# A four-layer graph network on one core: the masked minimum of a score tile taken in two halves of 512 columns

## What is computed

```python
# layer 0
h   = relu(fa[:, :, None, :] + fb[:, None, :, :])      # 1024 x 1024 pairs, 64 features
att = einsum('bijo,o->bij', h, W2)
att = softmax(att + where(adj > 0, 0.0, NEG_INF), axis=-1)
out = einsum('bij,bjc->bic', att, feat)
# layer 1: the same with leaky_relu(vu + iv), yita in the place of W2,
# and a small linear step behind it
```

## Time and profile before

| what | value |
|---|---|
| median of three runs | 5095.22 us |
| the profiled execution, its own time | 5096.0 us |
| its span in the trace | 5094.1 us |
| PE / DVE / ACT / POOL busy over the span | 4584.2 / 4798.2 / 4747.6 / 3856.7 us |
| TensorE's granted clock, mean | 0.983 of full |
| masked minima (L471) of tiles 0 to 127 start | 55.3 to 3460.2 us |

### The profile page before, as it was taken

The page is one execution under the profiler, slowest core; times in us unless marked ns, Lnnn a source line. Parts: engine busy times, 40 slices in busy tenths (PEclk is TensorE's granted clock), DMA queues, the critical chain, the costliest instruction groups (busy, mean ns, idle before and its releaser), DMA issues. The chain is left out here.

```text
span 5094.1 us, 118654 instructions
## 1 busy us (share of the span) xinstructions
PE 4584.2 (90%) x48920; PEld 1810.2 (36%) x48920; DVE 4798.2 (94%) x5489; ACT 4747.6 (93%) x5779; POOL 3856.7 (76%) x3611
## 2 busy tenths in 40 slices
PE   7888888888888999999999999998789999999998
PEld 2222222222222223232323323234445555555554
DVE  7999999999999999999999999996579999999998
ACT  7999999999999999999999999996779999999997
POOL 8999999999999999999999999993603223322333
PEclk9999999999999999999999999998879999999999
DMA  1000010000000000000000000003210111001100
GB/s 53 32 28 30 32 32 26 32 32 29 30 32 32 18 10 12 12 12 10 12 12 12 9 12 12 12 10 73 69 26 16 24 25 24 16 24 24 24 16 12
DMA packets 154140, 121.74 MB, mean 24 GB/s; under 512 B 118854, under 2 KB 120646, under 8 KB 153606
## 3 DMA queue, kind: packets, MB, share of 16 engines
q1 hardware_dynamic: 152902, 114.10, 8.0%
q10 hardware_dynamic: 704, 0.07, 0.0%
HBM read 86.87 MB, written 18.87 MB: 21 GB/s over the span
## 5 line engine op out<-in xcount | busy, mean ns | idle before, releaser
L200 POOL TENSOR_SCALAR a_hid_p<-a_BLOS,a_PHI,a_PLO 128x1024 f32<-128x1024 f32 x2720 | 3196.9, 1222 | 89.0 <-PE apsS L330 82.5
L459 DVE SCALAR_TENSOR_TENSOR a_hid_p<-apsB,a_THI,a_hid_p 128x1024 f32<-128x1024 f32 x2560 | 3074.7, 1273 | 16.5 <-POOL a_hid_p L200 14.6
L330 PE MATMUL apsS<-a_hid_p,a_sel_high 128*32 128x512 f32 x10880 | 2633.9, 597 | 169.9 <-ACT a_hid_a L367 96.9
L330 PE MATMUL apsS<-a_hid_a,a_sel_high 128*32 128x512 f32 x6144 | 1913.3, 597 | 47.1 <-ACT a_hid_a L367 24.9
L330 PE MATMUL apsS<-a_hid_a,a_sel_low 128*32 128x512 f32 x5504 | 1680.2, 597 | 109.1 <-ACT a_hid_a L367 61.7
L367 ACT ACTIVATE a_hid_a<-a_BHI,a_ALH 128x1024 f32<-128x1024 f32 x1536 | 1690.7, 1146 | 0.0
L367 ACT ACTIVATE a_hid_a<-a_BLO,a_ALH 128x1024 f32<-128x1024 f32 x1376 | 1534.6, 1146 | 0.0
L330 PEld LDWEIGHTS apsS<-a_hid_p,a_sel_high 128*32 128x32 f32 x10880 | 587.8, 109 | 938.5 <-issue 535.1
L761 PE MATMUL m3S<-xT,Q 64*128 64x512 f32 x2048 | 594.3, 655 | 28.1 <-ACT x_even L805 14.1
L330 PEld LDWEIGHTS apsS<-a_hid_a,a_sel_high 128*32 128x32 f32 x6144 | 419.7, 109 | 560.1 <-issue 303.7
L330 PEld LDWEIGHTS apsS<-a_hid_a,a_sel_low 128*32 128x32 f32 x5504 | 374.7, 109 | 647.9 <-issue 325.9
(11 more groups left out here) (187 smaller groups left out, 3870.7 us busy)
## 6 DMA issues: line engine op xcount, KB each, us to landing
a_adj_in<-adj SPq DMA_DIRECT2D x64, 512.0 KB, 3.7
mask_rows<-a_mask SPq DMA_DIRECT2D x64, 256.0 KB, 2.2
a_mask<-mask_rows SPq DMA_DIRECT2D x64, 256.0 KB, 2.7
maskb<-mask_rows SPq DMA_DIRECT2D x64, 256.0 KB, 3.0
mask<-mask_rows SPq DMA_DIRECT2D x64, 256.0 KB, 2.8
Xr<-x_odd SPq DMA_DIRECT2D x128, 64.0 KB, 2.1
out<-yn SPq DMA_DIRECT2D x64, 32.0 KB, 1.5
x_even<-x SPq DMA_DIRECT2D x1, 256.0 KB, 2.7
```

The lines of the kernel that those rows point to most:

```text
L200: gp.tensor_scalar(hid_p[:, at % RING_P, :], BLOS[:, g % 2, :], PHI[:, g % 2, m:m + 1], PLO[:, g % 2, m:m + 1], ALU.min, ALU.max).then_inc ...
L330: last = pe.matmul(psS[32 * q:32 * q + 32, h * HALF:(h + 1) * HALF], sel[:, 28 - 4 * p:60 - 4 * p], unit, start=s == 0 and layer == 0, sto ...
L459: dve.scalar_tensor_tensor(out=hid_p[:, at % RING_P, :], in0=psB[:, :], scalar=THI[:, g % 2, m:m + 1], in1=hid_p[:, at % RING_P, :], op0=A ...
```

## The change

`masked_min` becomes two operations of 512 columns. The first waits for a new semaphore `half_scored`, which the fourth matmul of the tile's last set raises, the second for `hid_used` as before. Each writes its row minimum to a column of its own (`half_lowest`), and a third VectorE operation, a 128x1 `tensor_tensor` with `min`, waits for both and writes `lowest(k)`; it raises `low_ready`, for which ScalarE's exponentials now wait. `min_ready` counts two for each tile. On TensorE, set 0 of the next tile and `key_term` wait for each half of the minimum in front of their own half. SyncE and GpSimd wait for the same event as before, by doubled counts.

```diff
@@ gpsimd / sync: the same event, counted twice
-                    gp.wait_ge(min_ready, k - 1)
+                    gp.wait_ge(min_ready, 2 * (k - 1))
@@ def key_term(k)
-                pe.wait_ge(min_ready, k)
                 for h, side in enumerate(halves):
+                    pe.wait_ge(min_ready, 2 * (k - 1) + h + 1)
@@ def hidden_set(k, s)
-                if s == 0 and k >= 1:
-                    pe.wait_ge(min_ready, k)
                 for h in range(n // HALF):
+                    if s == 0 and k >= 1:
+                        pe.wait_ge(min_ready, 2 * (k - 1) + h + 1)
                     for q, p, kind in units:
...
+                    if s == SETS - 1 and h == 0:
+                        last.then_inc(half_scored, 1)
                 last.then_inc(hid_used, 1)
@@ def exponentials(k)
-                act.wait_ge(min_ready, k + 1)
+                act.wait_ge(low_ready, k + 1)
@@ def masked_min(k)
-                dve.wait_ge(hid_used, (k + 1) * SETS)
+                dve.wait_ge(half_scored, k + 1)
...
-                dve.tensor_tensor_reduce(out=Z, in0=psS[:, :], in1=mask[:, k % 2, :], scale=1.0, scalar=-LOWEST,
-                                         op0=ALU.add, op1=ALU.min, accum_out=lowest(k)).then_inc(min_ready, 1)
+                for h in range(2):
+                    if h == 1:
+                        dve.wait_ge(hid_used, (k + 1) * SETS)
+                    dve.tensor_tensor_reduce(out=Z[:, columns(h)], in0=psS[:, columns(h)], in1=mask[:, k % 2, columns(h)],
+                                             scale=1.0, scalar=-LOWEST, op0=ALU.add, op1=ALU.min,
+                                             accum_out=half_lowest(k, h)).then_inc(min_ready, 1)
+                dve.wait_ge(min_ready, 2 * (k + 1))
+                dve.tensor_tensor(lowest(k), half_lowest(k, 0), half_lowest(k, 1), ALU.min).then_inc(low_ready, 1)
```

More of the change, by code:

```diff
@@ L63, in additive_layers @@
     lowest, halfc = lambda k: small[:, k % 2:k % 2 + 1], small[:, 8:9].to_broadcast([P, tiles])
+    half_lowest = lambda k, h: small[:, 2 + 2 * (k % 2) + h:3 + 2 * (k % 2) + h]
+    columns = lambda h: slice(h * HALF, h * HALF + HALF)
     per_tile = lambda ap: ap.rearrange("p (t c) -> p t c", c=C)
@@ L132, in additive_layers @@
         bounds_ready, keys_placed = sem("bounds_ready"), sem("keys_placed")
+        half_scored, low_ready = sem("half_scored"), sem("low_ready")
         turned, copied_low, copied_high = sem("turned"), sem("copied_low"), sem("copied_high")
@@ L153, in _ @@
                 else:
-                    sp.wait_ge(min_ready, k - 1)
+                    sp.wait_ge(min_ready, 2 * (k - 1))
                     sp.wait_ge(mask_stored[k % 2], 16 * (M // 2))
```

## The result

The changed kernel takes 5259.0 us (median of 4 runs, 5252.85 to 5259.97) where the kernel before takes 5093.16 (4 runs beside it): a ratio of 1.0316, 95% interval 1.0303 to 1.033. That is 166 us slower. The forecast was 5101, the range ended at 5119: the prediction is wrong, and not by a little.

The account below looks back on a forecast made before the run. The prediction took VectorE and ScalarE, in turns, as the bound: d of 0.25 us per minimum less waits given back, +4.3 us in layer 0 and +1.7 in layer 1, so 5095.2 + 6 = 5101 us; range 5088 to 5119.

Parts of the forecast that it names:

- What bounds the kernel: Layers 0 and 1: no engine alone; VectorE and ScalarE take turns in cycles of eight tiles, TensorE has slack.
- d: VectorE's added time per tile from minimum's start to next merged unit: +0.25 us, bounds +0.14 and +0.46.
- the early start: First half starts up to 0.86 us before `hid_used`; of a wait w the change takes back min(w, 0.61).
- TensorE's slack in layer 1: TensorE was said to have 19 to 26 us of slack in eight tiles of layers 0 and 1.
- The price of the halves, of the wait and of the 0.07 of the join: On VectorE: 0.61 first half, 0.69 to the second's end, 0.03 wait, 0.07 join; next merged unit at 1.40.
- Operations on one column take 0.14 and follow each other at 0.07: Price of the join on VectorE: from rows 10, next merged unit 0.07 us after the join's start.
- the upper bound of the join at 0.17: The join's share in the upper bound of d, 0.72 + 0.72 + 0.17 - 1.15 = +0.46 us.
- Rival B: VectorE's three pieces do not overlap, d = 0.46, costing places 3 to 7: +22 us, 5117; chance 0.25.
- Rival A: The join's wait on VectorE is free, d = 0.14: -3 us, 5092; chance 0.15.
- Rival C: All VectorE waits given back at the minimum are on the path: -19 us, 5076; chance 0.10.
- The signs I had named: Next merged unit at 1.40, minimum's idle under 30 us, ScalarE's exponential wait above 40, layer 0 cycle 216.0; other distance: wrong d.

Follow-up runs that it names:

- reduce_join: The changed kernel with the join as a tensor_reduce over one 128x2 SBUF input, not a tensor_tensor with two SBUF inputs: 5099.47 us, ratio to before 1.001.
- halves_late: reduce_join without the early start: both halves wait for `hid_used`, `half_scored` is gone; 5117.56 us, ratio 1.0051.
- chained: Two halves and no join: the second half waits for the first one's minimum and takes it as its initial value; 5105.81 us, ratio 1.0031.
- the pair of unused operations: The kernel before plus one unused 128x1 VectorE operation behind each minimum: two-input tensor_tensor 5228.34 us (1.026), tensor_reduce over two SBUF columns 5094.69 (1.0005).

## Why the prediction was wrong, point by point

**What bounds the kernel: right in the main.** VectorE and ScalarE take turns in cycles of eight tiles, and the early start does give back time on it. Three kernels that differ in d and in the early start came out near the sums built on this: reduce_join +6.1 us (forecast +6), halves_late +25 (20), chained +13.7 (12.4), the sums in brackets with the d of tile 29. The split by layer is less good. Layer 1 took +0.1, +11.4 and +4.0 us, where the sums say +1.7, +10 and +4.1; layer 0 took +6.6, +13.5 and +13.4, where they say +4.3, +10 and +8.3. In layer 0 something of 2 to 5 us is missing from the sum, so that +6.1 for a forecast of +6 is in part luck, and no run shows what. One reading of the rows was off: TensorE's slack in layer 1 is 214.60 - 196.63 = 18 us, not 19, on which nothing hangs.

**The price of the halves, of the wait and of the 0.07 of the join: right.** d of a join with one SBUF input is 0.25 at tile 29 and 0.27 in the median. The forecast of 5101 is the time of that kernel, 5099.5, and not of the changed one.

**The step that failed: "Operations on one column take 0.14 and follow each other at 0.07", used as the price of the join.** Those rows are from 14 us after the start, when GpSimd does not clamp units yet, and they have one input. I counted elements and fixed costs, and did not ask which memory each operand of the join is in and who else reads there at that moment. The trace of before has no VectorE operation with two SBUF inputs beside GpSimd's clamps, so it could not give the price. It did show the effect, in the later layers, where the masked minimum (L845) reads both its inputs from SBUF and GpSimd adds up heads (L695) once in a while. VectorE:

```profile
3785.34 1.22 DVE L845 CUSTOM_DVE_ANT_0 x_even<-x_even,mask 128x1024 f32<-128x1024 f32 x1
...
3786.47 1.75 DVE L845 CUSTOM_DVE_ANT_0 x_even<-x_even,mask 128x1024 f32<-128x1024 f32 x1
```

and GpSimd:

```profile
3785.50 1.63 POOL L695 TENSOR_TENSOR part<-prod 128x256 f32<-128x256 f32 x1 [91.85 <-DVE prod L880]
```

Of the 512 minima there, the 61 that start while such an addition runs take 1.74 to 1.75 us, the other 451 at most 1.23; and the 61 additions beside them take 1.6 us, the three without VectorE beside them 0.72. Since GpSimd clamps nearly without a pause where the join was to stand (210.19 of 215.47 us), these rows would have made the wait a rival. I had the upper bound of the join at 0.17, and its worst case is 8.96. The measured term: 1.6 us per tile on average, 0.44 in layer 0 and 2.7 in layer 1, of which most is on the path: the joins take 185 us more than those of reduce_join, the kernel 160.

The Trainium skill, "SBUF — State Buffer", sections "SBUF: two separate sides" and "Who interferes with whom", has the rule: a VectorE instruction with two SBUF inputs contends with a GpSimd instruction that reads SBUF, as its second input comes through a read interface that the two share, whichever is later blocks until the other's instruction is done; and `tensor_reduce` does not contend on this chip. The traces here agree on who contends (the pair of unused operations, 183.5 against 19.1 us). They go beyond it in how long: not for one clamp of 1.18 us but, where GpSimd has run for more than a dozen instructions, through up to seven or eight of them, until GpSimd pauses or its ring is full. Someone who had read that page for this change would have made "the join has to find a gap between GpSimd's clamps" a rival, with a price between one clamp, 1.2 us, per tile and the whole lead of the ring.

**Rival B** had the right sign with the wrong mechanism: the halves follow each other at 0.61 us, so they overlap as the operations before did. **Rival A**, the free wait, is refuted again: the join with one input starts 0.03 us behind the end of the second read (841.17 + 0.08 = 841.25, start 841.28), where the operation that doesn't wait starts ahead of the end. **Rival C** is refuted: with 38 us of idle time given back, reduce_join is not faster.

**The signs I had named** were fit to find it: the next merged unit at another distance than 1.40 (1.47 at tile 29, 9.27 from 2353.30 to 2362.57), ScalarE's wait far over 40.

## What to carry to other kernels

Before an operation is added beside a busy neighbour, list for each operand which memory it is in, not only how many elements it has: on this chip a VectorE operation with two SBUF inputs of a single column took ten times its own time on average, and over fifty times at worst, beside a GpSimd that hardly pauses. If the same can be computed from one SBUF operand (a reduction over adjacent columns) or with one in PSUM, it was free of that here. A price read from another part of the program holds only if the neighbours were as busy there as they will be here.

## What the runs showed of the hardware that was not expected

- Whether a VectorE operation with two SBUF inputs is let in at the end of GpSimd's current instruction goes with how long GpSimd has run without a pause: with at most 11 instructions done, in 375 of 376 cases; with 14 or more, it was held until GpSimd paused in all cases but one. The join from 2354.64 to 2362.65 passed six ends of clamps on its way.
- A pause of 0.10 us is enough, if it falls within a dozen GpSimd instructions ahead of VectorE's operation: one behind set 2 left the longest wait of layer 1 at 1.10 us, one behind set 8 at 8.07.
- GpSimd waits for VectorE as well: its addition L695 takes 1.6 us beside a minimum with two SBUF inputs and 0.72 alone.
- A minimum of 512 columns that reads its initial value from memory takes 751 ns on average, with an immediate one 686.
